# Last stage of a fused attention and FP4 feed-forward layer: another order of the per-tile steps on TensorE and ScalarE

## The reference

```python
x = _layernorm(x + attention(x))
gate = fp4_linear(x, w_gate)          # 256 -> 704
y    = fp4_linear(x, w_up)            # 256 -> 704
h    = silu(gate) * y
x    = _layernorm(x + fp4_linear(h, w_down))   # 704 -> 256
# fp4_linear quantises its input and its weight: per 16 values a scale max|.|/6,
# each value rounded to the grid 0, .5, 1, 1.5, 2, 3, 4, 6
```

## Time and profile before

| | |
|---|---|
| median of 3 runs | 3508.35 us (3505.88 to 3509.93) |
| profiled execution: its time, its span | 3508.1 us, 3506.3 us |
| span: PE busy | 3377.0 us (96%) |
| span: VectorE busy | 3217.4 us (92%) |
| span: ScalarE, GpSimd busy | 2665.2 us (76%), 761.1 us (22%) |
| mean granted TensorE clock | 0.982 |
| last stage | from about 2855 us to the end |

### The profile page before, as it was taken

How to read it: one execution, slowest core, us unless ns; L and a number is a source line. 1 busy time by engine, 2 the same in 40 slices (tenths; PEclk the granted TensorE clock), 3 DMA queues, 4 the chain that set the end, 5 groups by cost and what they waited for, 6 DMA issues and landing times.

```text
span 3506.3 us, 69112 instructions
## 1 busy us (share of the span) xinstructions
PE 3377.0 (96%) x27752; PEld 1518.8 (43%) x27752; DVE 3217.4 (92%) x3531; ACT 2665.2 (76%) x4946; POOL 761.1 (22%) x871
## 2 busy tenths in 40 slices
PE   7959999999999999999999999999999999999997
PEld 4523333333333333333333333333333346676665
DVE  5758999999999999999999999999999949988887
ACT  5624888888888888888888888888888874444444
POOL 5730110101011001101010110011000016655554
PEclk9977999999999999999999999999999999999999
DMA  5431222222221222212122221122111112211110
GB/s 151 169 122 43 103 92 80 80 103 98 82 79 60 83 80 100 82 43 77 64 83 82 86 82 60 61 82 77 61 65 68 45 44 61 83 47 40 38 35 22
DMA packets 132972, 264.18 MB, mean 75 GB/s; under 512 B 30022, under 2 KB 84518, under 8 KB 114214
## 3 DMA queue, kind: packets, MB, share of 16 engines
q1 hardware_dynamic: 123436, 251.38, 20.6%
q10 hardware_dynamic: 9216, 8.39, 0.7%
HBM read 173.11 MB, written 84.93 MB: 74 GB/s over the span
## 4 chain that ended last, share of the span: by engine, by line
PE 88%; ACT 5%; issue 3%; DVE 3%; DMA 1%; POOL 1%; SPq 0%; ACTq 0%; POOLq 0%; DVEq 0%
PE ps L686 36%; PE ps L739 32%; PE ps L822 8%; PE ps L834 4%; PE ps L659 3%; ACT arena L933 2%; PE ps L749 1%; PE ps L726 1%; PE ps L666 1%; ACT arena L908 1%; DVE arena L1074 1%; ACT v_all L981 1%; DMA arena<-in_xT 1%; ACT arena L971 0%; DVE arena L1134 0%
## 5 line engine op out<-in xcount | busy, mean ns | idle before, releaser
L1074 DVE TENSOR_REDUCE arena<-ps 128x1 f32<-128x1024 f32 x2048 | 2495.3, 1222 | 57.2 <-PE ps L686 40.9
L933 ACT ACTIVATE arena<-ps 128x512 f32<-128x512 f32 x4096 | 2222.1, 597 | 317.6 <-PE ps L726 232.5
L686 PE MATMUL ps<-kst,qst 48*128 48x512 f32 x4096 | 1517.0, 451 | 14.4 <-DVE arena L1074 14.3
L726 PE MATMUL ps<-qst,kst 51*128 51x512 f32 x4096 | 1496.0, 447 | 0.2
L739 PE MATMUL ps<-arena 128*32 128x256 f32 x16384 | 1308.2, 392 | 16.8 <-ACT arena L908 15.9
L686 PEld LDWEIGHTS ps<-kst,qst 48*128 48x128 f32 x4096 | 613.0, 187 | 870.3 <-DVE arena L1074 703.5
L739 PEld LDWEIGHTS ps<-arena 128*32 128x32 f32 x16384 | 326.1, 108 | 738.8 <-issue 406.8
L726 PEld LDWEIGHTS ps<-qst,kst 51*128 51x128 f32 x4096 | 607.6, 185 | 15.6 <-ACT arena L933 12.2
L1351 POOL TENSOR_TENSOR arena<-arena,ones 128x16 bf16<-128x16 f32 x64 | 14.2, 222 | 2302.2 <-DVE arena L1079 2302.2
L822 PE MATMUL ps<-wgT,arena 128*128 128x352 f32 x512 | 195.3, 463 | 15.5 <-ACT arena L923 15.5
L834 PE MATMUL ps<-wdT,arena 128*128 128x256 f32 (+1 forms) x768 | 181.1, 385 | 17.7 <-ACT arena L971 16.5
(11 more groups left out here) (104 smaller groups left out, 2086.4 us busy)
## 6 DMA issues: line engine op xcount, KB each, us to landing
qk_parts<-arena SPq DMA_DIRECT2D x32, 1024.0 KB, 6.4
kst<-qk_parts SPq DMA_DIRECT2D x128, 256.0 KB
qst<-qk_parts SPq DMA_DIRECT2D x128, 256.0 KB
qk_whole<-arena SPq DMA_DIRECT2D x16, 1024.0 KB, 5.9
arena<-qk_whole SPq DMA_DIRECT2D x16, 1024.0 KB, 5.1
kst<-qk_parts SPq DMA_DIRECT2D x128, 128.0 KB
qst<-qk_parts SPq DMA_DIRECT2D x128, 128.0 KB
att<-arena SPq DMA_DIRECT2D x256, 34.0 KB
```

Source lines behind the costliest of these rows:

```text
L686: mm = nc.tensor.matmul(ps[:, i % S_BANKS, :], q[SROW:SROW + STACK, qt * P:(qt + 1) * P], k[SROW:SROW + STACK, kc * CHUNK:(kc + 1) * CHUNK ...
L726: nc.tensor.matmul(ps[:, bank_of_t(g.c, i), :], kst[g.u % 2][first:first + ROWS, kb * P:(kb + 1) * P], qst[g.u % 2][first:first + ROWS, qb ...
L933: nc.scalar.activation(pt[kb % 2][:, qb * CHUNK:(qb + 1) * CHUNK], ps[:, bank_of_t(g.c, i), :], ACT.Exp).then_inc(p_ready, 1)
L1074: nc.vector.tensor_reduce(mx[g.u % 2][:, i // 2, i % 2:i % 2 + 1], ps[:, bank:bank + 2, :].rearrange("p b t -> p (b t)"), AX.X, ALU.max).t ...
```

## The change

In the last stage alone, the order in which TensorE and ScalarE go through their steps. No operation is added or removed, and no wait is changed. `gate_up` and `silu` are split so that each half is a stage of its own.

```diff
-            def gate_up(n):
-                pe.wait_ge(xhT_out, n.times(1, 1))
-                for hf in range(2):
-                    wait_after(pe, h_done, n.times(2, hf - 1))
...
+            def gate_up(n, hf):
+
+                if hf == 0:
+                    pe.wait_ge(xhT_out, n.times(1, 1))
+                wait_after(pe, h_done, n.times(2, hf - 1))
...
-            run_straight(TILES, [(7, xT_tile, 1), (1, proj, len(PROJ_AT)), (7, gate_up), (9, hT_tile), (9, down)])
+            run_straight(TILES, [(7, lambda n: gate_up(n, 0)), (9, hT_tile), (7, lambda n: gate_up(n, 1)),
+                                 (6, xT_tile, 1), (9, down), (0, proj, len(PROJ_AT))])
...
-            def silu(n):
-                wait_after(act, h_done, n.times(2, -2))
-                for hf in range(2):
-                    act.wait_ge(gu_psum, n.times(2, hf + 1))
...
+            def silu(n, hf):
+                if hf == 0:
+                    wait_after(act, h_done, n.times(2, -2))
+                act.wait_ge(gu_psum, n.times(2, hf + 1))
...
             run_straight(TILES, [
-                (6, norm1, 2), (14, norm2), (7, xT_out, 1), (14, store_out),
-                (6, steady_x, 2), (8, steady_h), (7, silu), (9, hT_out_of_psum)])
+                (14, norm2), (14, store_out), (6, steady_x, 2), (8, steady_h), (7, lambda n: silu(n, 0)), (9, hT_out_of_psum),
+                (7, lambda n: silu(n, 1)), (6, xT_out, 1), (5, norm1, 2)])
```

More of the change, by code:

```diff
@@ L814, in hT_tile @@
                     mm.then_inc(hT_psum, 1)
-            def gate_up(n):
-                pe.wait_ge(xhT_out, n.times(1, 1))
-                for hf in range(2):
-                    wait_after(pe, h_done, n.times(2, hf - 1))
[L820 to L824, removed]
+            def gate_up(n, hf):
+                if hf == 0:
+                    pe.wait_ge(xhT_out, n.times(1, 1))
+                wait_after(pe, h_done, n.times(2, hf - 1))
+                for ct in range(CT):
+                    for w, bank in ((wgT, 2 + 2 * hf), (wuT, 3 + 2 * hf)):
+                        mm = nc.tensor.matmul(ps[:, bank, 0:FH], xhT_r[n.u % 2][:, ct], w[:, ct, hf * FH:(hf + 1) * FH],
+                                              start=(ct == 0), stop=(ct == CT - 1))
+                mm.then_inc(gu_psum, 1)
             def down(n):
@@ L975, in hT_out_of_psum @@
                                      ).then_inc(hT_out, 1)
-            def silu(n):
-                wait_after(act, h_done, n.times(2, -2))
-                for hf in range(2):
-                    act.wait_ge(gu_psum, n.times(2, hf + 1))
-                    nc.scalar.activation(e_r[n.u % 2][:, hf * FH:(hf + 1) * FH], ps[:, 2 + 2 * hf, 0:FH], ACT.Silu
-                                         ).then_inc(e_done, 1)
+            def silu(n, hf):
+                if hf == 0:
+                    wait_after(act, h_done, n.times(2, -2))
+                act.wait_ge(gu_psum, n.times(2, hf + 1))
+                nc.scalar.activation(e_r[n.u % 2][:, hf * FH:(hf + 1) * FH], ps[:, 2 + 2 * hf, 0:FH], ACT.Silu
+                                     ).then_inc(e_done, 1)
             run_straight(TILES, [
-                (6, norm1, 2), (14, norm2), (7, xT_out, 1), (14, store_out),
-                (6, steady_x, 2), (8, steady_h), (7, silu), (9, hT_out_of_psum)])
+                (14, norm2), (14, store_out), (6, steady_x, 2), (8, steady_h), (7, lambda n: silu(n, 0)), (9, hT_out_of_psum),
+                (7, lambda n: silu(n, 1)), (6, xT_out, 1), (5, norm1, 2)])
             for c in range(4):
```

## The result

The changed kernel takes 3537.4 us (median of 6 runs, 3534.57 to 3545.47) against 3509.52 us before: ratio 1.0082, 95% interval 1.0069 to 1.0095. It is slower by 28 us, above the range of 3499 to 3524 us, and the cause is that of rival 1, the clock.

The account below looks back on a forecast made before the run. TensorE was taken to set the pace, VectorE 10% behind. Per group -2.00 - 1.03 + 3.03 = 0.00; with -3.6 at the end and +2.8 for the clock, 3508.1 us became 3507, range 3499 to 3524.

Parts of the forecast that it names:

- rival 1: TensorE's clock falls in many groups behind the 3.03 us wait: eight falls 3526 us, all 3543 us; chance 0.23.
- the tile of 9.06 us without waits: Last stage, TensorE: a tile takes 9.56 us, of which 0.50 is down's wait for ScalarE's copies of h.
- hT between the halves: Copies of h get gate_up's second half and xT_tile as cover: -0.50 us a tile, -2.00 a group.
- xT_out in front of norm1: The copy of turned x follows the second silu, so gate_up no longer waits for it: -1.03 us a group.
- The new wait in front of xT_tile: First tile of a group: TensorE waits for ScalarE's second copy of h before transposing x, +3.03 us a group.
- The zero that does not move: Group step: VectorE's variance end, taken as zero, stays; inverse_std's L1133 comes 3.03 us later, probably set by GpSimd.
- The end: From tile 58 on, no proj covers xT_out before the change; the new order saves 3.6 us there.
- The clock: Last stage, TensorE: one clock fall, at the last group's wait, +2.8 us; bounds 0 to +38 us.
- Rivals 2 to 4: Both waits go, none comes, 3465 (0.04); VectorE's chain shortens partly, 3485 (0.08); hT_tile gives only 0.26, 3513.5 (0.08).

Follow-up runs that it names:

- four added matmuls: Changed kernel plus four matmuls ahead of the second half of gate_up in the tile before each group: 3509.06 us, ratio 1.0001.
- the run with less rounding: Changed kernel with two added matmuls, GpSimd rounding only 16 of each 352 values of h in one tile of four: 3479.69 us, one run.
- one added matmul: Changed kernel plus one matmul ahead of the second half of gate_up in the tile before each group: 3532.5 us, ratio 1.0071.
- projection first: Changed kernel with the projection of tile s - 1 put in front of the transposes of x: 3521.94 us, ratio 1.0041.
- the last kernel shown: Changed kernel with projection before x's transposes, one hT_out count less, GpSimd's rounding held behind inverse_std in one tile of four: 3486.14 us, ratio 0.9928.

## Why the prediction was wrong

- *What bounds the kernel, and the tile of 9.06 us without waits.* Right. Undisturbed tiles of the changed kernel are 9.06 us apart (in its timeline, the loads of `xT_tile` at 3412.75 and 3421.81), and the late period of 39.15 us with four added matmuls is 0.12 below the 39.27 forecast. The four early periods were 0.4 above it; the forecast had no term for GpSimd's work there.
- *hT between the halves, and xT_out in front of norm1.* Right: both waits are gone.
- *The new wait in front of xT_tile, 3.03 us.* Right in place, size and the engine that ends it: 3.25 us at the load, 2.72 us by the modelled ends. The matmuls started 11.95 us behind `variance` (forecast 12.05).
- *The zero that does not move, because GpSimd's work sets it.* Right, and shown by the run with less rounding. I did not draw from it that this was the place to gain: one wait of GpSimd gave 12.9 us on the kernel before.
- *The end, -3.6 us.* Right where the clock stays up. From the last group's `variance` (3434.64) to the end the kernel with four added matmuls takes 70.35 us, against 71.55 before. 2.36 us of it are its added matmuls ahead of the last tile, where there is no wait to hide them (its row 3477.53, `PE L823`, to the next at 3479.89). An estimate without them is 67.99, 3.6 us less than before. The loads of the undisturbed tile in the changed kernel, and these two rows:

```profile
3412.75 0.14 PEld L757 LDWEIGHTS ps<-ident,arena 128*128 128x128 f32 x1
3421.81 0.14 PEld L757 LDWEIGHTS ps<-ident,arena 128*128 128x128 f32 x1
```

```profile
3477.53 2.53 PE L823 MATMUL ps<-wgT,arena 128*128 128x352 f32 x8
3479.89 0.76 PE L826 MATMUL ps<-wgT,arena 128*128 128x352 f32 x2
```

- *The clock.* This is the step that failed: "I take one". The count was wrong by more than ten: 13 of 13 periods had a fall, and so had the first group, and two more came behind the 13 periods. The price was too high: 2.75 us forecast from a fall that lasted from 82.72 to 89.56, 1.70 measured for one of 3.4 us. Without falls the sum was 3508.1 - 3.6 = 3504.5 us; with four added matmuls 3509.1 was measured, inside the range. Of the 4.6 us between, 2.4 are the added matmuls ahead of the last tile, 0.8 stand in the first 14 periods, and 1.4 are the kernel before, which took 3509.5 us in that session.
- The excess of 28 us, in the profiled executions from the end of the first group's `variance` to the end: 646.5 us against 620.8 before, 25.7 more. The first period gives 1.9 (40.22 against 38.33), the thirteen 23.7 (534.6 against 510.9), the rest 0.1. Against the four added matmuls the thirteen take 23.3 us more, and falls make up all of it: twelve of 1.7 us and the one of 6.8 us at half clock with 3.1 (its period is 42.78, its neighbour's there 39.63). Behind the thirteen, the end takes 71.7 us: two falls of 3.4 us (at 3485.4 and 3526.3) took back nearly all of the 3.6 us that it should have gained.
- The argument against rival 1 was that the wait was only 0.3 us longer than the 2.7 us after which the clock fell in the earlier trace rows. The distance from the last matmul to the fall was taken for the length of wait needed. In the changed kernel eleven of the thirteen falls came only when work had begun again, and in other kernels waits of 2.0 us brought some. One fall seen behind a wait of 4 us gave no lower bound. A single row was read as a threshold.
- *Rival 1* named the mechanism and, for a fall in every group, +35 us; +28 came. That the two are near each other is in part luck: it priced a fall at 2.75 us, where 1.7 was measured, and at the measured price 14 falls and the -3.6 give 20 us. There were 16 falls, one of them twice as long.
- *Rivals 2 to 4* did not occur.

## What to carry to other kernels

Waits that are spread over a period in small pieces can cost less than the same waits in one piece: the change kept 3.03 us of waiting in four tiles and only gathered it, and TensorE's clock did the rest. When a reordering moves a wait, price the longest single stretch without matmuls that it makes, and shorten it: by real work moved into it, and by looking for what holds the chain that ends it, on the engines off the path too. Here one wait of GpSimd for VectorE gave 12.9 us on the kernel before, where the new order by itself, with the clock held up, gave nothing.

## What the runs showed of the hardware

- Over the last stage of all kernels here, waits of TensorE of up to 1.86 us by the PE rows had no fall of the clock, those of 1.98 to 2.50 us had one in part of the cases, and those of 2.57 us and more had one each time. The same wait of 2.1 us brought a fall seven times in eight in one kernel (one added matmul) and five times in eight in another (projection first); what decides it stays open.
- In the thirteen periods of the changed kernel the clock fell 2.7 to 4.4 us behind the last matmul: from 0.4 us before work began again to 1.3 us after. It stayed down for 3.4 us in twelve of them and for 6.8 in one.
- Small f32 instructions of VectorE last longer beside GpSimd's elementwise ones, to within 0.04 us of their end: 0.65 us instead of 0.17 for the third of `inverse_std` on 8 columns, 0.89 instead of 0.19 for a scale instruction on 60. The tensor_reduce over 704 values lasted 0.88 us beside GpSimd's (3344.03, the last kernel shown) and 0.87 without (3396.07, the changed kernel).
